# Key blocks 0 and 1 of the value matmuls behind the maxima's transpose, key blocks 2 and 3 with the sums at place 8 of 12

## The chip, the cores and the metric

The kernel runs on one core of one Trainium2 chip. The metric is the device time of one execution in microseconds (us), lower is better. Three runs of the kernel before gave 889.77, 891.34 and 891.32 us, with a median of 891.32 us.

## The reference, cut to what matters

One transformer layer on x of 4 x 512 x 1024 floats: layer norm, attention with 32 query heads of width 32 that share one key and one value head, a position bias and a causal mask, output projection, residual; then layer norm, a linear layer with unpacked integer weights, residual.

```python
q = (hidden_states @ Wq).reshape(b, s, NUM_HEADS, HEAD_DIM)
kv = hidden_states @ Wkv
k, v = (kv[..., :HEAD_DIM], kv[..., HEAD_DIM:])
scores = jnp.einsum('bqhd,bkd->bhqk', q, k) * scale
scores = jnp.where(causal[None, None], scores + bias[None], -jnp.inf)
attn = jax.nn.softmax(scores, axis=-1)
out = jnp.einsum('bhqk,bkd->bqhd', attn, v).reshape(b, s, h)
return out @ Wo
```

## The kernel before, in words

Three stages follow one another: projections of the four batches (to about 257 us of the profile), attention (about 257 to 570 us), and output projection with the linear layer, tile by tile. The change lies in attention.

Attention has 32 steps (`STEPS`), one for four heads of one batch. Each engine has its own program, written out by hand; a semaphore wait is the only thing that lets one engine wait for another, and each engine works through its list in order. In step s TensorE (PE) issues, in `attend(s)` (L644), twelve places (`RING`), 0 to 11:

- at every place but 2, one transposed score matmul (`score_t`, L609) into one of three PSUM banks of `p_st`, for step s. Places 0, 1, 3 and 4 are key block 0 of the four heads (512 columns), 5 to 8 key block 1 (384 columns), 9 and 10 key block 2 for two heads each, 11 key block 3 for all four (512 columns each). It waits until ScalarE has taken the exponential of the place three before it (`free_bank`, L585).
- at place 2, the transpose of the row maxima of step s+1 (`turn_max`, L599). It waits for the last maximum of that step and, as it uses the same three banks, for the exponential of place 11 of step s-1.
- after either, two, one or one plain score matmuls (`score`, L582) for the heads two steps ahead, of 128 and 256, then 384, then 512 columns. VectorE takes their row maxima (L948). Four scores make a head; a bank of `p_s` is written again once the maximum of the head before has been taken.
- at the places of two tables, the matmuls of step s-1 that multiply the exponentials by the values (`values`, L620, key block `kb`) and by the ones that sum them (`totals`, L633). These are plain fp32 matmuls with 32 columns of weights, in four column tiles at once (`128*32` in the profile, while all others show `128*128`). The profile shows eight records for four such instructions.

```python
VALUES_AT = {1: (0,), 4: (1,), 6: (2, 3)}
TOTALS_AT = {9: (0, 1)}
```

ScalarE (ACT) takes the exponentials of the eleven places in order (L789) into `pt`. Its program has three other operations in a step: the high part of the negated maxima (`max_high`, L781) between places 1 and 3, the copy of step s-1's output out of PSUM (`take_o`, L796) right behind the exponential of place 9, and in steps 2 to 17 one half-row cast of the output weights (`wo_high`, L805) right behind the exponential of place 10.

```python
if k == 8 and s > 0:
    take_o(s - 1)
if k == 9 and 0 <= s - 2 < HALVES:
    wo_high(s - 2)
```

VectorE (DVE) takes the sixteen maxima, then the low part of the transposed maxima (`max_low`, L955), the weights' low part (L965) in steps 3 to 18, and four reciprocals (L961), one behind each 256-column maximum, in steps 10 to 13, 18 to 21 and 26 to 29. GpSimd (POOL) cuts the exponentials at the diagonal (`cut`, L439) and adds key blocks before the sums (`add`, L446, L452). SyncE (SP) issues all DMAs in order: in each step the four loads of queries three steps ahead (`load_q`), the two stores of the maxima (`store_max`, L310, which the next step's first `score_t` waits for), the store of the output (`store_o`, L316, which waits for `take_o`), and one load of weights; in step 26 also five loads for the next stage.

Of the kernel before, what the change touches and what calls it, by code (L numbers as in the profile page):

```python
# [75 lines left out]
def layer(nc, x, wq, wkv, wo, qweight, w_scale, w_zero, bias, kpos, slopes, out, qh_d, ql_d, ext_d, wi_d, inv_d, o_d):  # L76

    ctx = ExitStack()
    with ctx:
# [433 lines left out]
        def _(pe):  # L513
# [98 lines left out]
            def values(s, kb):  # L612
                b = s // GROUPS
                if kb == 0:
                    at_least(pe, o_taken, s)
                    if s == 0:
                        pe.wait_ge(q_freed, CK * B + 2)
                pe.wait_ge(cut_done, 4 * s + kb + 1)
                for h in range(4):
                    last = pe.matmul(p_o[32 * h:32 * h + 32, kb * P:S], vst[:, TPB * b + kb, :],  # L620
                                     pt[s % 2][:, h, PT_AT[kb]:PT_AT[kb] + KB_LEN[kb]], start=(kb == 0), stop=(kb == 3),
                                     tile_position=(0, 32 * h), skip_group_check=True)
                if kb == 3:
                    last.then_inc(v_done, 1)

            def totals(s, part):
                b, g = s // GROUPS, s % GROUPS
                if part == 0:
                    at_least(pe, sums_taken, b if g == 0 else 0)
                    pe.wait_ge(add_done, 2 * s + 2)  # L630
                at, to = ((ADD_AT, slice(0, S)), (PT_AT[3], slice(2 * P, 3 * P)))[part]
                for h in range(4):
                    last = pe.matmul(p_sum[32 * h:32 * h + 32, to], pick[:, 7 - g:39 - g],  # L633
                                     pt[s % 2][:, h, at:at + to.stop - to.start], start=(g == 0 and part == 0),
                                     stop=(g == GROUPS - 1 and part == 1), tile_position=(0, 32 * h), skip_group_check=True)
                if part == 1:
                    last.then_inc(pv_done, 1)

            VALUES_AT = {1: (0,), 4: (1,), 6: (2, 3)}
            TOTALS_AT = {9: (0, 1)}  # L640

            FIRST_AT = {4: 0, 6: 1, 8: 2, 10: 3}

            def attend(s):  # L644
                n = 4 * (4 * s + AHEAD)
                for at in range(RING):
# [8 lines left out]
                    if s > 0:  # L655
                        for kb in VALUES_AT.get(at, ()):
                            values(s - 1, kb)
                        for part in TOTALS_AT.get(at, ()):
                            totals(s - 1, part)
# [468 lines left out]
```

## Time and profile before

| | us |
|---|---|
| median of three runs | 891.32 |
| lowest, highest run | 889.77, 891.34 |
| the profiled execution | 891.1 |
| its span, first to last instruction | 889.3 |
| TensorE busy | 850.5 (96%) |
| VectorE busy | 536.4 (60%) |
| ScalarE busy | 331.8 (37%) |
| GpSimd busy | 390.4 (44%) |
| mean granted TensorE clock | 0.991 |
| each step from 2 to 26, and 28 and 29 | 9.56 to 9.67 |
| steps 0, 1, 27, 30 | 10.80, 12.00, 10.90, 8.38 |
| step 18 (433.21 to 442.79): SP issues the maxima stores at | 436.82 and 437.37 |
| step 18: SP issues the output store at | 441.56 |

The span is that of the one profiled execution; 1.8 us of its time lie outside it. Busy shares are means over the three stages. The chain of waits is the work followed back from the last instruction. A step is read from the timeline: it begins where its first `score_t` starts. TensorE's records overlap, so the time that an instruction takes of the engine is the distance to the start of the next, not its own length.

### The profile page before, as it was taken

The numbers are of one execution on the slowest core, as the hardware profiler recorded it, in microseconds if no ns is written. First come the engines' busy times: TensorE is split into PE (matmuls) and PEld (weight loads), VectorE is DVE, ScalarE is ACT, GpSimd is POOL, SyncE is SP. The second block draws the span as 40 slices with busy tenths as digits, with TensorE's granted clock in tenths as the row PEclk, the third lists the DMA queues.
The fourth block names the chain that finished last, engine by engine and source line by source line (L and its number), as shares of the span: only waits on it lengthen the run. The fifth ranks groups of instructions, "written<-read, shape, count | busy, mean of one in ns | idle before, by whom it ended". The sixth has DMA issues, their size and how long they took to land.

```text
span 889.3 us, 13953 instructions
## 1 busy us (share of the span) xinstructions
PE 850.5 (96%) x4912; PEld 620.6 (70%) x4912; DVE 536.4 (60%) x1527; ACT 331.8 (37%) x647; POOL 390.4 (44%) x254
## 2 busy tenths in 40 slices
PE   2789999999989999999999999999999999999997
PEld 2578888888865555555555555578888888888885
DVE  6455253542575788888887777356655455555535
ACT  2323122222135767767766656422112112111211
POOL 1000000000016888888888888855443333444211
PEclk9989999999998999999999999999999999999999
DMA  5445554449443664666665572574344533334211
GB/s 160 145 157 154 166 160 145 138 133 219 137 119 89 154 150 124 153 145 142 147 150 154 157 182 76 156 187 119 96 117 130 127 100 107 95 95 117 73 48 48
DMA packets 90110, 117.19 MB, mean 132 GB/s; under 512 B 9060, under 2 KB 51044, under 8 KB 89960
## 3 DMA queue, kind: packets, MB, share of 16 engines
q1 hardware_dynamic: 90040, 116.30, 49.3%
q8 instruction: 39, 0.64, 0.3%
q14 instruction: 31, 0.25, 0.1%
HBM read 76.95 MB, written 38.93 MB: 130 GB/s over the span
## 4 chain that ended last, share of the span: by engine, by line
PE 89%; DVE 3%; DMA 3%; ACT 2%; SPq 1%; POOL 1%; issue 1%; DVEq 0%; ACTq 0%
PE p_o L529 19%; PE p_st L692 13%; PE p_s L677 10%; PE p_st L609 10%; PE p_o L677 9%; PE p_o L620 9%; PE p_s L582 9%; PE p_o L633 4%; PE p_st L529 2%; PE p_s L522 1%; DMA xt<-ml 1%; DMA raw<-in_wq_dram 1%; PE p_st L599 1%; PE p_s L706 1%; PE p_st L706 1%
## 5 line engine op out<-in xcount | busy, mean ns | idle before, releaser
L948 DVE CUSTOM_DVE_ANT_0 spill<-p_s,mask 128x128 bf16<-128x128 f32 (+3 forms) x512 | 224.2, 482 | 69.1 <-PE p_s L582 66.5
L439 POOL TENSOR_SCALAR_AFFINE_SELECT pt<-pt 128x512 f32<-128x512 f32 x128 | 83.1, 662 | 302.8 <-ACT pt L789 302.8
L789 ACT ACTIVATE pt<-p_st 128x512 f32<-128x512 f32 (+1 forms) x352 | 178.3, 560 | 90.5 <-PE p_st L609 90.2
L529 PE MATMUL p_o<-xt,wqh 128*128 128x512 f32 x512 | 170.1, 398 | 2.2 <-DVE wql L1058 2.2
L582 PE MATMUL p_s<-kst,xt 98*128 98x128 f32 (+3 forms) x512 | 149.7, 331 | 0.0
L609 PE MATMUL p_st<-xt,kst 100*128 100x512 f32 (+1 forms) x352 | 142.2, 408 | 6.1 <-DMA xt<-ml 4.6
L529 PEld LDWEIGHTS p_o<-xt,wqh 128*128 128x128 f32 x512 | 97.1, 190 | 22.8 <-DVE wql L1058 2.6
L446 POOL TENSOR_TENSOR pt<-pt 128x1536 f32<-128x1536 f32 x32 | 111.7, 3490 | 2.7
L582 PEld LDWEIGHTS p_s<-kst,xt 98*128 98x128 f32 x512 | 99.5, 195 | 11.9 <-DVE mx L948 0.9
L529 PE MATMUL p_o<-xt,wql 128*128 128x512 f32 x256 | 100.5, 392 | 0.0
L609 PEld LDWEIGHTS p_st<-xt,kst 100*128 100x128 f32 x352 | 66.9, 191 | 43.2 <-DVE ml L955 18.3
L462 POOL TENSOR_TENSOR osl<-ob,osh 128x1024 fp32r<-128x1024 f32 x14 | 33.6, 2403 | 134.2 <-ACT osh L825 134.1
L620 PE MATMUL p_o<-pt,vst 128*32 128x512 f32 (+3 forms) x1024 | 89.8, 445 | 0.0
L692 PE MATMUL p_st<-wi,yth 128*128 128x512 f32 x256 | 82.1, 397 | 2.2 <-DVE yo L1023 2.2
L692 PE MATMUL p_st<-wi,ytl 128*128 128x512 f32 x256 | 82.1, 397 | 0.0
L452 POOL TENSOR_TENSOR pt<-pt 128x1024 f32<-128x1024 f32 x32 | 76.4, 2387 | 0.0
L933 DVE TENSOR_TENSOR ql<-p_o,qh 128x512 fp32r<-128x512 f32 x32 | 22.1, 691 | 75.6 <-ACT qh L762 75.5
L762 ACT CAST qh<-p_o 128x512 fp32r<-128x512 f32 x32 | 18.8, 587 | 125.8 <-PE p_o L529 125.7
L469 POOL TENSOR_TENSOR xr<-xr,bias_b 128x1024 f32<-128x1024 f32 x16 | 50.6, 3161 | 30.8 <-ACT y L834 30.8
L692 PEld LDWEIGHTS p_st<-wi,yth 128*128 128x128 f32 x256 | 48.1, 188 | 14.1 <-issue 2.6
L842 ACT CAST yth<-p_s 128x512 fp32r<-128x512 f32 x16 | 9.4, 588 | 126.1 <-PE p_s L706 126.1
L692 PEld LDWEIGHTS p_st<-wi,ytl 128*128 128x128 f32 x256 | 48.2, 188 | 11.7
(104 smaller groups left out, 1205.1 us busy)
## 6 DMA issues: line engine op xcount, KB each, us to landing
xt<-qh_d SPq DMA_DIRECT2D x64, 256.0 KB
xin<-in_x_dram SPq DMA_DIRECT2D x16, 512.0 KB, 3.9
qh_d<-qh SPq DMA_DIRECT2D x32, 256.0 KB, 2.6
ql_d<-ql SPq DMA_DIRECT2D x32, 256.0 KB, 3.2
xt<-ql_d SPq DMA_DIRECT2D x32, 256.0 KB
o_d<-o_st SPq DMA_DIRECT2D x32, 256.0 KB, 2.8
ob<-o_d SPq DMA_DIRECT2D x64, 128.0 KB, 4.1
inv_b<-inv_d SPq DMA_DIRECT2D x64, 128.0 KB, 4.6
```

The source lines that it names most:

```text
L439: pool.affine_select(out=own, in_=own, compare_op=ALU.is_ge, fill=0.0, base=0, pattern=[[0, 4], [1, P]], channel_multiplier=-1).then_inc(c ...
L446: pool.tensor_tensor(p[:, :, ADD_AT:ADD_AT + 3 * P], p[:, :, PT_AT[0] + P:PT_AT[0] + S], p[:, :, PT_AT[1]:PT_AT[1] + 3 * P], ALU.add).then ...
L452: pool.tensor_tensor(to, to, p[:, :, PT_AT[2]:PT_AT[2] + 2 * P], ALU.add).then_inc(add_done, 1)
L469: pool.tensor_tensor(xr[:, t % 2, :], xr[:, t % 2, :], bias_b[:, :], ALU.add).then_inc(res_bias, 1)
L529: last = pe.matmul(dst, w[:, c, cols], xs[:, c, :], start=(c == 0 and k == 0), stop=(c == CK - 1 and k == 2))
L582: pe.matmul(scores_of(n), qst[s % 4][0:R_MAX, j, qb * P:(qb + 1) * P], kst[0:R_MAX, b * S:b * S + keys], start=True, stop=True).then_inc(s ...
L609: pe.matmul(p_st[:, place(k) % 3, 0:heads * KB_LEN[kb]], kst[0:R_END, b * S + kb * P:b * S + (kb + 1) * P], qst[s % 4][0:R_END, j:j + head ...
L620: last = pe.matmul(p_o[32 * h:32 * h + 32, kb * P:S], vst[:, TPB * b + kb, :], pt[s % 2][:, h, PT_AT[kb]:PT_AT[kb] + KB_LEN[kb]], start=(k ...
L677: last = pe.matmul(p_wo[t % 2][:, n, :], a[:, c, :], w[:, c, n * S:(n + 1) * S], start=(c == 0 and k == 0), stop=(c == CK - 1 and k == 2))
L692: last = pe.matmul(p_ff[:, n, :], a[:, c, :], wi[:, c, n * S:(n + 1) * S], start=(c == 0 and low == 0), stop=(c == CK - 1 and low == 1))
L789: act.activation(pt[s % 2][:, j:j + heads, PT_AT[kb]:PT_AT[kb] + KB_LEN[kb]], p_st[:, place(k) % 3, 0:heads * KB_LEN[kb]].rearrange("p (j ...
L948: dve.tensor_tensor_reduce(spill[:, SPILL_AT[qb]:SPILL_AT[qb] + keys], scores_of(n), mask[:, S - keys:S], 1.0, LOWEST, ALU.add, ALU.max, m ...
```

## The change

Two tables move the value matmuls and the sums to other places of the step. Nothing is added or removed.

```diff
-            VALUES_AT = {1: (0,), 4: (1,), 6: (2, 3)}
-            TOTALS_AT = {9: (0, 1)}
+            VALUES_AT = {2: (0, 1), 8: (2, 3)}
+            TOTALS_AT = {8: (0, 1)}
```

TensorE, places 0 to 4 of a step. L609 is `score_t`, L582 `score`, L620 `values`, L599 the transpose. Before:

```order
L609 MATMUL p_st<-xt,kst 128x512
L582 MATMUL p_s<-kst,xt 128x384
L620 MATMUL p_o<-pt,vst 32x512 x4
L599 MATMUL p_st<-ident,mx 128x128
L582 MATMUL p_s<-kst,xt 128x512
L609 MATMUL p_st<-xt,kst 128x512
L582 MATMUL p_s<-kst,xt 128x128
L582 MATMUL p_s<-kst,xt 128x256
L609 MATMUL p_st<-xt,kst 128x512
L582 MATMUL p_s<-kst,xt 128x384
L620 MATMUL p_o<-pt,vst 32x384 x4
```

The same places now:

```order
L609 MATMUL p_st<-xt,kst 128x512
L582 MATMUL p_s<-kst,xt 128x384
L599 MATMUL p_st<-ident,mx 128x128
L582 MATMUL p_s<-kst,xt 128x512
L620 MATMUL p_o<-pt,vst 32x512 x4
L620 MATMUL p_o<-pt,vst 32x384 x4
L609 MATMUL p_st<-xt,kst 128x512
```

The value matmuls of key block 0 stood ahead of the transpose and now stand behind it and the score that follows it; those of key block 1 come up from place 4.

TensorE, places 8 to 10, before (L633 is `totals`):

```order
L609 MATMUL p_st<-xt,kst 128x384
L582 MATMUL p_s<-kst,xt 128x512
L609 MATMUL p_st<-xt,kst 128x512
L582 MATMUL p_s<-kst,xt 128x128
L582 MATMUL p_s<-kst,xt 128x256
L633 MATMUL p_o<-pt,pick 32x512 x4
L633 MATMUL p_o<-pt,pick 32x128 x4
L609 MATMUL p_st<-xt,kst 128x512
```

Now:

```order
L609 MATMUL p_st<-xt,kst 128x384
L582 MATMUL p_s<-kst,xt 128x512
L620 MATMUL p_o<-pt,vst 32x256 x4
L620 MATMUL p_o<-pt,vst 32x128 x4
L633 MATMUL p_o<-pt,pick 32x512 x4
L633 MATMUL p_o<-pt,pick 32x128 x4
L609 MATMUL p_st<-xt,kst 128x512
L582 MATMUL p_s<-kst,xt 128x128
L582 MATMUL p_s<-kst,xt 128x256
```

Key blocks 2 and 3 leave place 6 and, with the sums, stand between the matmuls of place 8 and the `score_t` of place 9.

ScalarE's list is the same in both kernels. From the exponentials of places 5 to 8 on it reads, in steps 2 to 17:

```order
L789 ACTIVATE pt<-p_st 128x384 x4
L789 ACTIVATE pt<-p_st 128x2x256
L796 COPY o_st<-p_o 128x512
L789 ACTIVATE pt<-p_st 128x2x256
L805 CAST woh<-ob 128x512
```

The first `128x2x256` is place 9, whose `score_t` now comes behind the sums, and the copy of the output still follows it.

## Rows read from the trace of the kernel before

**Rows 1.** Window of step 18: length, busy PE, PEld, DVE, ACT, POOL; clock, DMA share, GB/s
```profile
433.20:442.78 9.58, 9.58 (x77) 5.67 (x76) 8.51 (x39) 6.74 (x15) 8.27 (x7) 1.00 0.61 143
```

**Rows 2.** Timeline of PE, step 18: start us, us, engine, line, operation, count
```profile
433.44 0.40 PE L582 MATMUL p_s<-kst,xt 98*128 98x128 f32 x2
433.68 0.41 PE L609 MATMUL p_st<-xt,kst 100*128 100x512 f32 x1
433.93 0.34 PE L582 MATMUL p_s<-kst,xt 98*128 98x384 f32 x1
434.19 1.06 PE L620 MATMUL p_o<-pt,vst 128*32 128x512 f32 x8
435.19 0.33 PE L599 MATMUL p_st<-ident,mx 128*128 128x128 f32 x1
435.27 0.48 PE L582 MATMUL p_s<-kst,xt 98*128 98x512 f32 x1
435.59 0.40 PE L609 MATMUL p_st<-xt,kst 100*128 100x512 f32 x1
...
438.36 0.86 PE L620 MATMUL p_o<-pt,vst 128*32 128x256 f32 x16
439.15 0.44 PE L609 MATMUL p_st<-xt,kst 100*128 100x384 f32 x1
...
440.59 1.28 PE L633 MATMUL p_o<-pt,pick 128*32 128x512 f32 x16
441.80 0.50 PE L609 MATMUL p_st<-xt,kst 100*128 100x512 f32 x1
442.13 0.34 PE L582 MATMUL p_s<-kst,xt 98*128 98x384 f32 x1
442.32 0.40 PE L609 MATMUL p_st<-xt,kst 100*128 100x512 f32 x1
442.55 0.40 PE L582 MATMUL p_s<-kst,xt 98*128 98x512 f32 x1
```

**Rows 3.** Timeline of DVE, around the start of step 18
```profile
433.05 0.56 DVE L948 CUSTOM_DVE_ANT_0 spill<-p_s,mask 128x384 bf16<-128x384 f32 x1 [0.95 <-PE p_s L582]
433.53 0.69 DVE L948 CUSTOM_DVE_ANT_0 spill<-p_s,mask 128x512 bf16<-128x512 f32 x1
434.14 0.29 DVE L948 CUSTOM_DVE_ANT_0 spill<-p_s,mask 128x128 bf16<-128x128 f32 x1
...
434.69 0.35 DVE L961 RECIPROCAL sums<-sums 128x32 f32<-128x32 f32 x1
434.96 0.50 DVE L948 CUSTOM_DVE_ANT_0 spill<-p_s,mask 128x384 bf16<-128x384 f32 x1
```

**Rows 4.** Timeline of all engines in step 0, a score that waits for a maximum
```profile
262.24 0.08 DVE L948 DVE_READ_ACCUMULATOR2_ANT mx<- 128x1 f32 x1
...
262.37 0.19 PEld L582 LDWEIGHTS p_s<-kst,xt 98*128 98x128 f32 x1 [0.31 <-DVE mx L948]
...
262.71 0.40 PE L609 MATMUL p_st<-xt,kst 100*128 100x512 f32 x1
```

**Rows 5.** Timeline of ACT, around the ends of steps 17 and 18
```profile
433.25 0.61 ACT L805 CAST woh<-ob 128x512 fp32r<-128x512 f32 x1
433.76 1.57 ACT L789 ACTIVATE pt<-p_st 128x512 f32<-128x512 f32 x3
...
440.95 0.58 ACT L796 COPY o_st<-p_o 128x512 f32<-128x512 f32 x1
442.33 1.09 ACT L789 ACTIVATE pt<-p_st 128x512 f32<-128x512 f32 x2 [0.80 <-PE p_st L609]
```

**Rows 6.** Chain of waits, 515 to 531 us (steps 26 and 27): start us, us, what
```profile
517.57 0.59 ACT o_st L796
...
524.30 6.05 DMA xt<-ml
```

**Rows 7.** Timeline of PE, the sums in step 30
```profile
556.20 1.28 PE L633 MATMUL p_o<-pt,pick 128*32 128x512 f32 x16 [1.13 <-POOL pt L452]
```

## The prediction

> **What bounds it now.** The page shows TensorE busy for 96% of the span. I read one step of attention next, by the sums over windows and the timeline. Step 18 takes 9.58 us, all of it busy on TensorE, with VectorE at 8.51, GpSimd at 8.27 and ScalarE at 6.74 [rows 1]. By the table above, the steps from 2 to 29 all take 9.56 to 9.67 us, except step 27 (10.90). So the step is TensorE's issue time, and what the others hold back is hidden, by 1.07 us in VectorE's case. Two questions decide: what the new order saves of the 9.58, and whether the two other engines, fed in larger lumps, still keep up.
>
> **What the order saves.** Durations are distances between starts [rows 2]. Plain matmuls cost 0.24 us for 512 columns (442.32 to 442.55), 0.18 for 384 (442.13 to 442.32), 0.24 for a 128 and a 256 together (433.44 to 433.68). A column-tiled group costs more than its columns: key blocks 2 and 3 (384 columns) take 0.79 (438.36 to 439.15), the sums (640 columns) 1.21 (440.59 to 441.80). The 256 columns between them cost 0.42, or 1.67 ns each, so each group has 0.15 fixed. The matmul ahead takes 0.08 more than its form (433.93 to 434.19, 0.26 for 0.18), the one behind 0.10 more (441.80 to 442.13, 0.33 for 0.24). That is 0.33 us for one group. Behind key block 0 stands the transpose, which with the slower start of its follower costs 0.17 (0.08 to 435.27, then 0.32 for 0.24). Now: four groups, 4 x 0.23 + 3 x 0.10 = 1.22, plus the transpose. After: two groups, 0.66. Both sides keep 0.17 for the transpose. **Saved: 0.56 us a step**, leaving 9.02 us of issue. Over 29 steps this is 16 us if nothing waits.
>
> The Trainium skill, TensorEngine Tiling (Array Packing), Key Properties, says that changing the tiling mode drains TensorE. That rule speaks for the change and its sign agrees with the fixed costs above.
>
> **What waits between places 3 and 8.** These six places now run without a pause: two heads of scores with six `score_t`. Count from the start of place 3. TensorE reaches the last score of place 8 after 0.33 (place 3, behind a group) + 0.24 + 0.24 + 0.18 + 0.18 + 0.24 + 0.18 + 0.24 + 0.18 + 0.18 + 0.18 = 2.37 us. It must wait for the 512-column maximum of the head before. VectorE starts on a score 0.31 us after it has streamed (the score at 442.13 has streamed at 442.32 [rows 2]; one step of 9.58 earlier that is 432.74, and VectorE starts at 433.05 [rows 3]) and its first pair here has streamed at 0.57. From 0.88 on it needs 0.55 for the pair (434.14 to 434.69), 0.48 for 384 and 0.61 for 512 columns (433.05, 433.53, 434.14) [rows 3], so the head is through at 2.52; reading the result takes 0.08, and TensorE goes on 0.05 later (262.24, 262.37) [rows 4], at 2.65. Wait 0.28. A waiting matmul also shows its weight load: from 262.37 to the next matmul at 262.71 are 0.34 for a form of 0.24 [rows 4], +0.10. **Cost: 0.4 us a step**, and 0.26 more where a reciprocal lies between (434.69 to 434.96 [rows 3]). In the old order two groups of 0.79 us stood here, and VectorE caught up in them.
>
> **What waits between place 9 and the next transpose.** Count from the start of place 9. Unhindered, TensorE reaches the transpose at 0.33 + 0.24 + 0.24 + 0.18 + 0.24 + 0.24 + 0.24 + 0.24 + 0.24 + 0.18 = 2.37 us. ScalarE used to take the exponential of place 9 and the output's copy (440.95) while TensorE did the sums, then sat idle for 0.80 us [rows 5]. Now place 9 comes behind the sums: ScalarE is idle during them, for 1.9 us of group, and starts at 0.53 (441.80 to 442.33). Then it has place 9, the copy, place 10, in steps 2 to 17 the cast, and place 11, at 0.49 us each (three take 1.57 and the last of them 0.60) and 0.51 for the cast (433.25 to 433.76) [rows 5]. Place 10 ends at 0.53 + 2 x 0.49 + 0.60 = 2.11, and place 1 of the next step needs its bank, where TensorE arrives at 1.95: with 0.05 to notice, 0.21 of wait and 0.10 of load, so the transpose would be reached at 2.68. Place 11 ends at 0.53 + 3 x 0.49 + 0.60 = 2.60, with the cast 3.11, and the transpose needs that: 2.65, or **3.16 with the cast**. VectorE allows it at 2.65, with a reciprocal 2.91. The old order hid this wait behind key block 0, which stood ahead of the transpose: VectorE was done at 434.14 + 0.08 [rows 3, 4], and the transpose came at 435.19 [rows 2]. So the loss is 0.31 us plain, 0.54 with a reciprocal, 0.79 with the cast.
>
> **By step** (a step pays for its own places 3 to 8, and at its transpose for the step before): plain, 9.02 + 0.38 + 0.31 = 9.71; with the cast 9.02 + 0.38 + 0.79 = 10.19; a reciprocal in places 3 to 8 adds 0.26, one ahead of the transpose 0.23 if there is no cast. Against 9.58:
> - cast alone, steps 3 to 9 and 14 to 17: 11 x 0.61 = 6.7
> - cast and reciprocals, 10 to 13 and 18: 5 x 0.87 = 4.4
> - reciprocals at both points, 19 to 21 and 27 to 29: 6 x 0.62 = 3.7
> - at one point, 22 and 26: 2 x 0.37 = 0.7
> - plain, 2 and 23 to 25: 4 x 0.13 = 0.5
> - step 1, whose transpose waits for nothing new: -0.2; step 0 has no groups and stays.
>
> Together +15.8 us.
>
> **Step 27 and the queues.** SP's list is unchanged, but its output store waits for the copy, which now ends about 1.6 us after place 9 starts, that is 0.15 us into the next step; before it ended at 440.95 + 0.58 [rows 5], 1.26 us ahead of it. The query loads behind it slip by about 1 us. Maxima stores are issued about 4 us into a step (the table), and the longest landing took 6.05 us [rows 6]; in steps of 10 us that is covered. It is not in step 27, where five more loads stand in SP's queue: from the copy's end at 518.16 to the landing at 530.35 are 12.2 us [rows 6], so the step lasts about 12.3 instead of 10.9. That is 0.8 beyond what it got above. GpSimd (8.27 of 9.58) gets the same spacing in longer steps, and its last sum for step s-1 is ready well ahead of place 8, so I cost it at nothing. Step 30 has no scores; its sums waited 1.13 us for GpSimd [rows 7], and now the copy and place 9 come behind them: +0.5 (bounds 0 and 1.5). In step 31 the projection pieces keep their places: 0 (bounds -1 and +1). Sum: **+17 us**, rounded. A larger load exposure is possible, since four matmuls in a step may pay it, some of them hidden in a later wait: I take +18.
>
> The profiled execution took 891.1 us (span 889.3), in line with the median of 891.32. Forecast: **909.0 us**, 2% slower. The skill's same page, under PSUM Bottleneck, warns that tiling speeds TensorE up but not the copies out of PSUM, which may become the bottleneck. No row can show that of tiling as such, yet it is the kind of limit that the sums find.
>
> **Rivals.** *All waits hidden.* If ScalarE and VectorE kept up as they do now, the 16 us of saved drains would be whole: 875 us. For it: TensorE is busy through all of step 18 [rows 1]. Against it: [rows 3, 5] put both engines' ends behind TensorE's arrival at three points. It decides the sign: below 0.56 us of waits a step the change is faster. 6%. By the skill's rule on drains alone the time would be about this one.
>
> *ScalarE has slack that I don't see*, and only VectorE's pace counts: 0.38 + 0.31 a step, 0.49 more in the twelve steps with reciprocals, gives 28 x 0.13 + 12 x 0.49 = +9.5 and the step 27 and 30 terms, about 902 us. For it: ScalarE is busy only 6.74 of 9.58. Against: the order of its list. 17%.
>
> *The maxima land late.* With the query loads next to the maxima stores, landing as late as 6.05 us after issue in every step, plain steps grow to 10.1 and others slightly, some 4 to 8 us more: 916 us. 12%.
>
> *My sum*, within 5 us: 62%. The last 3% are no change, where saving and waits balance.
>
> **Range and chances.** The terms' bounds (loads exposed or not, 0.1 us at two points of 29 steps, 6 us; step 30 and 31, 3 us) and the rivals on both sides give 900 to 918. Faster by over 0.2% (about what a measurement can tell from no change) 0.06, within 0.03, slower 0.91.
>
> **What would show it.** Right: steps near 10.2 us in 3 to 17 and 9.7 in 23 to 25; the transpose's weight load waiting for `pt` L789 in steps 3 to 18; scores of 512 columns at place 8 waiting for `mx` L948; ScalarE idle for 1.5 us or more ahead of place 9, not ahead of place 10; two groups a step with 0.15 fixed each. Wrong: steps of 9.1 to 9.3 us, or a transpose that waits for nothing.

## The result, and the profile after

The changed kernel takes 911.79 us (median of 4 runs, 908.19 to 912.85) where the kernel before takes 890.55 (4 runs, 889.52 to 891.34). The ratio is 1.0232, 95% interval 1.0201 to 1.0263: slower by 2.3%. The forecast was 909.0 us in a range of 900 to 918.

The profiled execution has a span of 906.4 us, 17.1 more than the one of before. The first lines of its page:

```profile
span 906.4 us, 13953 instructions
PE 860.4 (95%) x4912; PEld 620.6 (68%) x4912; DVE 528.7 (58%) x1527; ACT 320.2 (35%) x647; POOL 399.0 (44%) x254
```

The number of instructions is the same. The mean granted clock is 0.992, where it was 0.991, so the clock is no part of these 17.1 us. It is part of the distance between the medians, 21.2 us: the other three executions of the changed kernel have spans of 909.9 to 911.1 us at a mean granted clock of 0.987 to 0.989, and the span multiplied by the clock is 899.2 to 899.9 us in all four. The profiled execution is the fastest of them, and the remaining 4 us go with the clock.

The loss lies in attention, step by step. These are windows of four steps of the changed kernel: step 5 (with the weights' cast), 12 (cast and reciprocals), 21 (reciprocals) and 24 (neither). The columns are those of [rows 1].

```profile
309.86:320.19 10.33, 9.88 (x77) 5.71 (x77) 7.63 (x35) 6.32 (x15) 8.63 (x7) 1.00 0.56 132
382.60:393.15 10.55, 10.09 (x77) 5.61 (x77) 8.37 (x39) 6.38 (x15) 8.85 (x7) 1.00 0.52 128
475.97:486.15 10.18, 10.11 (x78) 5.69 (x77) 7.78 (x40) 5.86 (x14) 8.27 (x7) 1.00 0.54 134
505.95:515.78 9.83, 9.80 (x77) 5.49 (x77) 6.95 (x36) 5.80 (x14) 8.28 (x7) 1.00 0.60 152
```

All four were 9.58 us or within 0.02 of it. TensorE's busy column hides most of the loss: in the last of these steps it is 9.80 of 9.83 us, though the step is 0.25 us longer than before. A matmul that waits a little is drawn longer. The timeline of TensorE in step 5, which answers to [rows 2]:

```profile
309.86 0.40 PE L609 MATMUL p_st<-xt,kst 100*128 100x512 f32 x1
310.10 0.45 PE L582 MATMUL p_s<-kst,xt 98*128 98x128 f32 x2
310.58 0.50 PE L609 MATMUL p_st<-xt,kst 100*128 100x512 f32 x1
310.92 0.33 PE L582 MATMUL p_s<-kst,xt 98*128 98x384 f32 x1
311.67 0.30 PE L599 MATMUL p_st<-ident,mx 128*128 128x128 f32 x1 [0.42 <-DVE mx L948]
311.73 0.48 PE L582 MATMUL p_s<-kst,xt 98*128 98x512 f32 x1
312.14 1.71 PE L620 MATMUL p_o<-pt,vst 128*32 128x512 f32 x16
313.78 0.50 PE L609 MATMUL p_st<-xt,kst 100*128 100x512 f32 x1
...
316.12 0.34 PE L609 MATMUL p_st<-xt,kst 100*128 100x384 f32 x1
316.45 0.50 PE L582 MATMUL p_s<-kst,xt 98*128 98x512 f32 x1
316.88 0.86 PE L620 MATMUL p_o<-pt,vst 128*32 128x256 f32 x16
317.56 1.26 PE L633 MATMUL p_o<-pt,pick 128*32 128x512 f32 x16
318.75 0.50 PE L609 MATMUL p_st<-xt,kst 100*128 100x512 f32 x1
```

The two groups are there: 0.41 us from the score ahead to the first value matmul, then 1.64 (312.14 to 313.78) and 1.87 (316.88 to 318.75), with the fixed cost once each. Three waits are there too. At place 1 TensorE starts 0.48 us after the pair of scores (310.10 to 310.58) where the pair costs 0.24. The transpose comes 0.75 us after a score of 0.18 (310.92 to 311.67). The last score of place 8 comes 0.33 us after a `score_t` of 0.18 and costs 0.43 itself. What ends that last wait, in the timeline of all engines:

```profile
316.31 0.08 DVE L948 DVE_READ_ACCUMULATOR2_ANT mx<- 128x1 f32 x1
...
316.45 0.19 PEld L582 LDWEIGHTS p_s<-kst,xt 98*128 98x128 f32 x1 [0.31 <-DVE mx L948]
```

It is the maximum of the head before, read out at 316.39, 0.06 us ahead of the weight load: the same picture as in step 0 of before [rows 4], now in every step from 2 to 29. The scores of places 6 and 7 wait too, for 0.1 us or less (315.36 to 315.70 for a pair of 0.24), since VectorE is behind all along this stretch.

ScalarE's timeline around the end of step 4, against [rows 5]:

```profile
305.32 1.33 ACT L789 ACTIVATE pt<-p_st 128x384 f32<-128x384 f32 x3
308.95 0.60 ACT L789 ACTIVATE pt<-p_st 128x512 f32<-128x512 f32 x1 [2.29 <-PE p_st L609]
309.45 0.58 ACT L796 COPY o_st<-p_o 128x512 f32<-128x512 f32 x1
309.91 0.62 ACT L789 ACTIVATE pt<-p_st 128x512 f32<-128x512 f32 x1
310.40 0.63 ACT L805 CAST woh<-ob 128x512 fp32r<-128x512 f32 x1
310.90 1.60 ACT L789 ACTIVATE pt<-p_st 128x512 f32<-128x512 f32 x3
```

It sits idle for 2.29 us during the second group, then has place 9, the copy, place 10, the cast and place 11 in a row. In the kernel before it idled for 0.80 us behind the copy, with the copy done. The waits of steps 2 to 30 in sum (engine, line waited for: us, times, longest), and then the first two of the kernel before, steps 2 to 29:

```profile
ACT pt L789 <- PE p_st L609: 116.7, 60, 2.3
DVE spill L948 <- PE p_s L582: 72.2, 68, 1.6
POOL pt L439 <- ACT pt L789: 48.2, 58, 1.6
```

```profile
ACT pt L789 <- PE p_st L609: 74.0, 111, 1.1
DVE spill L948 <- PE p_s L582: 48.6, 84, 1.1
```

Two engines that wait 117 and 72 us for TensorE, more than before, still make TensorE wait: they idle while the groups run and are late when the scores come.

### The profile page after: what moved, and what is told of

Read it like the earlier page. It is cut to its first block, busy times and chain, and to the rows that moved or that the text cites. A ratio compares the mean times of both kernels' runs of the same rounds, so it can differ in the third digit from the quotient of the medians.

```text
span 906.4 us, 13953 instructions
## 1 busy us (share of the span) xinstructions
PE 860.4 (95%) x4912; PEld 620.6 (68%) x4912; DVE 528.7 (58%) x1527; ACT 320.2 (35%) x647; POOL 399.0 (44%) x254
## 4 chain that ended last, share of the span: by engine, by line
PE 84%; DVE 5%; DMA 4%; issue 3%; ACT 2%; SPq 1%; DVEq 0%; ACTq 0%
PE p_o L529 19%; PE p_st L692 13%; PE p_o L677 10%; PE p_s L677 10%; PE p_s L582 8%; PE p_o L620 8%; PE p_st L609 7%; PE p_o L633 3%; DMA xt<-ml 3%; PE p_st L529 2%; DVE spill L948 2%; PE p_s L522 1%; DMA raw<-in_wq_dram 1%; PE p_st L599 1%; PE p_s L706 1%
## 5 line engine op out<-in xcount | busy, mean ns | idle before, releaser
L948 DVE CUSTOM_DVE_ANT_0 spill<-p_s,mask 128x128 bf16<-128x128 f32 (+3 forms) x512 | 220.8, 482 | 90.9 <-PE p_s L582 90.1
L439 POOL TENSOR_SCALAR_AFFINE_SELECT pt<-pt 128x512 f32<-128x512 f32 x128 | 89.0, 707 | 313.5 <-ACT pt L789 313.5
L789 ACT ACTIVATE pt<-p_st 128x512 f32<-128x512 f32 (+1 forms) x352 | 175.7, 570 | 133.7 <-PE p_st L609 132.1
L582 PE MATMUL p_s<-kst,xt 98*128 98x128 f32 (+3 forms) x512 | 158.5, 349 | 0.1
L609 PE MATMUL p_st<-xt,kst 100*128 100x512 f32 (+1 forms) x352 | 141.5, 406 | 8.7 <-DMA xt<-ml 4.5
L582 PEld LDWEIGHTS p_s<-kst,xt 98*128 98x128 f32 x512 | 94.0, 192 | 29.4 <-DVE mx L948 19.2
L609 PEld LDWEIGHTS p_st<-xt,kst 100*128 100x128 f32 x352 | 66.5, 189 | 49.4 <-issue 25.7
L620 PE MATMUL p_o<-pt,vst 128*32 128x512 f32 (+3 forms) x1024 | 83.5, 443 | 0.0
L692 PEld LDWEIGHTS p_st<-wi,yth 128*128 128x128 f32 x256 | 48.2, 188 | 14.1 <-issue 2.6
L620 PEld LDWEIGHTS p_o<-pt,vst 128*32 128x32 f32 x1024 | 26.8, 110 | 41.0 <-issue 28.9
```

The costliest lines, as they stand in the source:

```text
L439: pool.affine_select(out=own, in_=own, compare_op=ALU.is_ge, fill=0.0, base=0, pattern=[[0, 4], [1, P]], channel_multiplier=-1).then_inc(c ...
L582: pe.matmul(scores_of(n), qst[s % 4][0:R_MAX, j, qb * P:(qb + 1) * P], kst[0:R_MAX, b * S:b * S + keys], start=True, stop=True).then_inc(s ...
L609: pe.matmul(p_st[:, place(k) % 3, 0:heads * KB_LEN[kb]], kst[0:R_END, b * S + kb * P:b * S + (kb + 1) * P], qst[s % 4][0:R_END, j:j + head ...
L692: last = pe.matmul(p_ff[:, n, :], a[:, c, :], wi[:, c, n * S:(n + 1) * S], start=(c == 0 and low == 0), stop=(c == CK - 1 and low == 1))
L789: act.activation(pt[s % 2][:, j:j + heads, PT_AT[kb]:PT_AT[kb] + KB_LEN[kb]], p_st[:, place(k) % 3, 0:heads * KB_LEN[kb]].rearrange("p (j ...
L948: dve.tensor_tensor_reduce(spill[:, SPILL_AT[qb]:SPILL_AT[qb] + keys], scores_of(n), mask[:, S - keys:S], 1.0, LOWEST, ALU.add, ALU.max, m ...
```

## Which engine holds the transpose

The profile puts the transpose's wait of 0.42 us down to a maximum of VectorE. My sum had put it down to ScalarE's exponential of place 11 in the steps with a cast. VectorE's timeline says when the last of the 16 maxima was ready:

```profile
310.33 0.69 DVE L948 CUSTOM_DVE_ANT_0 spill<-p_s,mask 128x512 bf16<-128x512 f32 x1
310.94 0.08 DVE L948 DVE_READ_ACCUMULATOR2_ANT mx<- 128x1 f32 x1
...
311.50 0.08 DVE L948 DVE_READ_ACCUMULATOR2_ANT mx<- 128x1 f32 x1
```

It was ready at 311.02, 0.65 us ahead of the transpose; place 11's exponential ended at about 310.90 + 0.62 = 311.52. Two semaphores, one label. VectorE had meanwhile gone on to the next head, and a maximum that the transpose does not need was read out at 311.58, just behind the exponential. That fits the label: it seems to name whichever semaphore went up last. In step 11, where a reciprocal delays that later maximum, the same wait carries ScalarE's name, as it does in steps 12 to 14:

```profile
373.88 0.30 PE L599 MATMUL p_st<-ident,mx 128*128 128x128 f32 x1 [0.41 <-ACT pt L789]
```

Theory S is my sum: ScalarE's list holds the transpose in steps 3 to 18, VectorE just behind it. Rival V believes the label. Rival L says that the late landings of the maxima make the loss. Three kernels tell them apart: the changed kernel with the copy moved, with the cast moved, and with both. Microseconds against the changed kernel are differences of medians from two sets of runs, in which the kernel before had 890.55 and 892.18 us (892.83 and 892.57 in the later sets), and the executions of one kernel differ by their clock. So they are good to 3 us at best; the step lengths, read from one trace each, are the sharper measure.

**The copy behind the exponential of place 8**

```diff
-                    if k == 8 and s > 0:
+                    if k == 7 and s > 0:
                         take_o(s - 1)
```

> The changed kernel with ScalarE's copy of the output moved from behind the exponential of place 9 to behind that of place 8, into its idle time during the value matmuls and sums. Theory S (the chain of ScalarE's list after place 9 holds the transpose in steps 3 to 18; without it VectorE's maxima hold it, 0.5 us earlier): steps 4 to 9 go from 10.33 to about 9.85 us, steps 11 to 13 from 10.54 to about 10.35, steps 23 and 24 stay at 9.8; the output store leaves earlier, so the late landings in steps 18, 25 and 27 go too. Time down by 8 to 11 us against the changed kernel. Rival V (VectorE's pace alone sets the transpose, as the profile's label on that wait says): steps 4 to 9 stay at 10.33. Rival L (late landings of the maxima make most of the loss): steps 4 to 9 stay, and only steps 18, 25 and 27 shrink, 3 us in all.

Measured: 900.89 us (4 runs, ratio to before 1.0090, 1.0069 to 1.0112), 10.9 us less than the changed kernel. Steps 4 to 9 take 9.84 or 9.85 us, steps 11 to 13 10.18 or 10.19, steps 23 and 24 9.77 or 9.78. Steps 18, 25 and 27 have lost their extra time (10.05, 9.77, 10.19). Its window of step 5, and then the timelines of TensorE, VectorE and ScalarE around the transpose:

```profile
309.24:319.08 9.84, 9.62 (x77) 5.61 (x76) 7.55 (x37) 6.44 (x15) 8.64 (x7) 1.00 0.58 136
```

```profile
310.56 0.30 PE L599 MATMUL p_st<-ident,mx 128*128 128x128 f32 x1 [0.22 <-ACT pt L789]
```

```profile
309.71 0.69 DVE L948 CUSTOM_DVE_ANT_0 spill<-p_s,mask 128x512 bf16<-128x512 f32 x1
310.32 0.08 DVE L948 DVE_READ_ACCUMULATOR2_ANT mx<- 128x1 f32 x1
```

```profile
309.81 1.58 ACT L789 ACTIVATE pt<-p_st 128x512 f32<-128x512 f32 x3
```

The two ends now lie within 0.02 us of each other: the maximum is read out at 310.32 + 0.08 = 310.40, place 11's exponential, the first of the three, ends at 309.81 + 0.60 to 0.62, about 310.42. Rival V is out: nothing on VectorE changed, and the step fell by 0.49 us, one copy. Rival L is out for these steps.

**The cast behind the exponential of place 8**

```diff
-                    if k == 9 and 0 <= s - 2 < HALVES:
+                    if k == 7 and 0 <= s - 2 < HALVES:
```

> The changed kernel with ScalarE's cast of the output weights moved from behind the exponential of place 10 to behind that of place 8. Theory S: steps 4 to 9 go from 10.33 to about 9.8, steps 11 to 13 to about 10.3, all steps from 19 on stay as they are, since they have no cast; time down by about 7 us. Rival V: steps 4 to 9 stay at 10.33, time unchanged. Rival L: nothing changes.

Measured: 905.14 us (ratio 1.0139, 1.0115 to 1.0163), 6.7 us less than the changed kernel. Most of steps 5 to 9 take 9.78 to 9.83 us, steps 11 to 13 10.10 to 10.19. Steps 20 and 21 are within 0.1 us of the changed kernel's. So far as expected; but steps 23, 26 and 28 took 10.33, 10.48 and 11.31 us in this execution (changed kernel 9.82, 9.90 and 9.67), where no change was expected. These are waits for the maxima's landing, and in step 28 also the clock, on which more below.

**Both**, that is, the two edits above together

> The changed kernel with both the copy and the cast behind the exponential of place 8. Theory S: no better than the copy alone (within 2 us of it), since VectorE then holds the transpose at 2.65 us after place 9 and either move takes ScalarE below that: steps 4 to 9 about 9.85. A rival in which ScalarE's list is the only limit: the two gains add, steps 4 to 9 go to about 9.4 us and the time by a further 7 us.

Measured: 898.69 us (ratio 1.0070, 1.0044 to 1.0097), 2.2 us less than with the copy alone; steps 4 to 9 take 9.77. The gains of 10.9 and 6.7 don't add: they end at the same wall, VectorE. In step 5 the maximum is read out at 310.09 + 0.08 = 310.17 and the transpose starts at 310.23, while place 11's exponential ended 0.5 us earlier; and steps with and without a cast are now equally long (9.77). A little over the 2 us that I had allowed is left; the steps account for 1.1 of them, 0.07 us in each step with a cast.

## VectorE's pace, and what the order really saves

**Reciprocals cut short**

```diff
-                of = slice(part * 32, part * 32 + 32)
+                of = slice(part * 32, part * 32 + (1 if b < B - 1 else 32))
```

> The changed kernel with the reciprocals of the first three batches cut from 32 columns to 1 (31 of 32 columns of the sums stay as they are, so the output differs). Theory S: VectorE's pace counts in places 3 to 8 and, without the cast, at the transpose: steps 11 to 13 go from 10.54 to about 10.4, steps 20 and 21 from 10.18 to about 9.9, steps 4 to 9 stay at 10.33. Time down 3 to 5 us. Rival (ScalarE alone): no step changes.

The kernel leaves out 31 of every 32 columns of these reciprocals. Measured: 908.50 us (ratio 1.0192, 1.0159 to 1.0224), 3.3 us less than the changed kernel. Steps 10 to 13 fall from 10.54 to 10.39 or 10.40, step 20 from 10.19 to 10.02, step 21 from 10.18 to 9.76; steps 4 to 9 stay at 10.33. VectorE does count, by these steps; the time alone would not show it, since the two ratios' intervals overlap, and the profiled span is 906.5 us, like the changed kernel's 906.4: steps 27 and 28 took 1.0 and 1.5 us longer here, by a later landing of the maxima and the clock behind it.

**Maxima over the last 128 keys only**, with copy and cast behind place 8. It leaves the other keys out of the row maxima.

```diff
-                keys = (qb + 1) * P
-                dve.tensor_tensor_reduce(..., scores_of(n),
+                keys = P
+                dve.tensor_tensor_reduce(..., scores_of(n)[:, qb * P:qb * P + P],
```

> The changed kernel with copy and cast behind place 8 and, besides, every row maximum taken over the last 128 keys only (the other keys are left out of the maxima, so the output differs). VectorE then needs about 0.2 us for each score in place of 0.2 to 0.6. Theory S (two groups in place of four save 0.56 us of issue a step, and waits for VectorE are all that is left in the way): steps of 9.0 us throughout, with at most 0.05 us between those with and without cast or reciprocals; time about 16 us below the kernel before (12 to 18). Rival (the drains that were counted as saved are paid elsewhere, or PE's own queue holds it): steps stay above 9.4 us.

Measured: 875.13 us (4 runs, 873.47 to 877.05; ratio 0.9799, 0.9776 to 0.9822), 17.4 us below the kernel before. Most steps take 8.93 to 8.96 us, with or without cast; the long ones are steps 2 and 26 (9.14 each), where the transpose waits for a maximum, steps 10 and 27 (9.36, 10.52), behind which TensorE idles for 0.27 and 1.42 us until the maxima land, and step 28 (10.68), of which more below. Against the kernel with both moves only the maxima differ, and step 5 falls from 9.77 to 8.95: those 0.82 us were VectorE's. The window of step 5, and TensorE around its transpose:

```profile
307.78:316.73 8.95, 8.95 (x77) 5.63 (x76) 4.81 (x35) 6.38 (x15) 8.24 (x7) 1.00 0.66 152
```

```profile
308.49 0.34 PE L582 MATMUL p_s<-kst,xt 98*128 98x384 f32 x1
308.66 0.27 PE L599 MATMUL p_st<-ident,mx 128*128 128x128 f32 x1
308.69 0.47 PE L582 MATMUL p_s<-kst,xt 98*128 98x512 f32 x1
309.09 1.71 PE L620 MATMUL p_o<-pt,vst 128*32 128x512 f32 x16
```

This is the saving with nothing in its way: 9.58 - 8.95 = 0.63 us a step, where I had worked out 0.56. The difference is the transpose. I had charged it 0.17 on both sides; between two plain matmuls it starts 0.17 after a score of 0.17 and its follower 0.03 later, and the next interval is 0.40, of which 0.24 are the score, 0.08 the lead into the group, 0.08 its own tail: 0.11 in all. The fixed cost belongs to the column-tiled groups, not to the transpose.

## Each half of the change alone

```diff
-            VALUES_AT = {2: (0, 1), 8: (2, 3)}
-            TOTALS_AT = {8: (0, 1)}
+            VALUES_AT = {2: (0, 1), 6: (2, 3)}
+            TOTALS_AT = {9: (0, 1)}
```

> The front half of the change alone: key blocks 0 and 1 at place 2, key blocks 2 and 3 at place 6 and the sums at place 9 as before. Theory S: one group less saves about 0.3 us a step, but the transpose now waits for VectorE and ScalarE (the copy is still done during the sums, so in steps with the cast for about 0.3 to 0.6 us, in others 0.2 to 0.4): steps 9.7 to 9.85 us, time 3 to 7 us above the kernel before. Rival (the back half alone makes the loss): steps of about 9.3 us, time 7 to 9 us below the kernel before.

Measured: 895.73 us (10 runs, ratio 1.0041, 1.0026 to 1.0056). Steps 4 to 9 take 9.82 to 9.84, steps 19 to 25 9.62 to 9.64.

```diff
-            VALUES_AT = {2: (0, 1), 8: (2, 3)}
+            VALUES_AT = {1: (0,), 4: (1,), 8: (2, 3)}
```

> The back half of the change alone: key block 0 at place 1 and 1 at place 4 as before, key blocks 2 and 3 with the sums at place 8. Theory S: one group less saves 0.33 us a step, but the copy now stands in ScalarE's list behind place 9 and after the sums; place 1 waits 0.2 to 0.3 us for the exponential of place 10, the transpose is hidden behind key block 0 as before except where the cast stands ahead of it, and places 5 to 8 run short of VectorE by 0.1 to 0.3 us: steps of about 9.6 to 9.8 us, time 3 to 8 us above the kernel before, with a late landing in step 27. Rival (the front half alone makes the loss): steps of about 9.25 us, time 9 us below the kernel before.

Measured: 901.04 us (4 runs, ratio 1.0105, 1.0072 to 1.0138), 8.2 above the kernel before in its own set of runs, just over the 3 to 8 that I had expected. Steps lie between 9.55 and 9.94 for the most part. Its weight loads name the landing of the maxima 13 times:

```profile
PEld p_st L609 <- DMA xt<-ml: 11.5, 13, 3.6
```

Late landings are not what this half loses by, though: steps without one (6 to 8, 18, 19) take 9.79 to 9.81 us, 0.22 more than before, which is 6 us over attention.

Each half loses, 0.4% and 1.1%, and the whole loses more than their sum (2.3%): with the front half alone the copy is still done during the sums, with the back half alone the transpose is still covered by key block 0. Together neither cover is left. This reading of the two halves is argued from the order of the lists; that each loses and that they more than add is measured.

**Key blocks 0 and 1 ahead of the transpose**

```diff
-            VALUES_AT = {2: (0, 1), 8: (2, 3)}
+            VALUES_AT = {1: (0, 1), 8: (2, 3)}
```

> As the changed kernel, but key blocks 0 and 1 stand at place 1, ahead of the transpose, and so hide its wait. Theory S: the transpose waits for nothing (its weight load is free 1.5 us before its turn), but place 3 onward still runs short of VectorE, now by a little more, since the group no longer lets VectorE finish the 512-column score of place 2, and ScalarE's copy still delays places 1 and 3: steps of 9.7 to 10.0 us without the step in time between steps with and without the cast being over 0.1 us, time 15 us above the kernel before (10 to 17). Rival (the transpose's wait is the whole loss): steps of about 9.1 us, faster than the kernel before by over 10 us.

Measured: 909.39 us (ratio 1.0191, 1.0155 to 1.0226), 16.6 above the kernel before; steps 6 to 9 take 10.01, like steps 22 to 24 without the cast (10.00 to 10.02). The transpose's wait is gone and so is the 0.5 us between steps with and without a cast. The loss is not: in step 22 TensorE's loads now wait at place 1 for ScalarE (0.22 us), at place 5 for the low part of the maxima, which comes behind the later transpose (0.59 us, with TensorE itself idle for 0.22), and at place 8 for a maximum (0.31 us). Steps 25, 27 and 28 took 11.37, 12.17 and 11.45 us, behind late landings of the maxima and, in step 28, at a lower clock.

## The maxima's landing

```diff
-                if s > 0:
-                    store_o(s - 1)
+                if s > 1:
+                    store_o(s - 2)
```

and `store_o(STEPS - 2)` behind the loop.

> The changed kernel with SP's output store of a step issued one step later, behind the stores of the maxima, so that neither the query loads nor the maxima wait for the copy. Theory S: the steps with waits for the maxima's landing (18, 25, 27 and 1.1 us in 27 as before) lose them: step 18 goes from 11.1 to about 10.5, step 25 from 10.7 to 9.8, step 27 from 11.3 to about 10.3; steps 4 to 9 stay at 10.33. Time down 2 to 3 us. Rival L (landing also holds the other steps): steps 4 to 9 fall below 10.2 and the time by over 5 us.

Measured: 908.76 us (ratio 1.0192, 1.0161 to 1.0222), 3.0 below the changed kernel, which is not clear of noise: the intervals overlap. Step 18 takes 10.52 where it took 11.11, step 25 9.81 for 10.73, step 27 10.19 for 11.34; steps 4 to 9 stay at 10.33. What stood in the changed kernel at the end of step 18, in the chain of waits and in TensorE's timeline, against [rows 6]:

```profile
448.99 7.10 DMA xt<-ml
```

```profile
456.13 0.50 PE L609 MATMUL p_st<-xt,kst 100*128 100x512 f32 x1 [0.40 <-DMA xt<-ml]
```

So rival L holds for three steps, not for the rest. What it is worth in sum is less than these steps show, 2.7 us: in the changed kernel the steps behind them, 19, 26 and 28, took only 9.66, 9.90 and 9.67, since ScalarE and VectorE caught up while TensorE stood; here they take 10.19, 10.17 and 10.18. That gives 1.3 us back, and 1.4 remain.

A long wait for the landing may cost a second time. In four of the kernels above (cast moved, reciprocals cut short, short maxima, key blocks ahead of the transpose) TensorE idled for 1.42 to 2.28 us ahead of step 28, and in the step that followed its granted clock fell. The window of the value matmuls of key blocks 0 and 1 in step 28, short maxima:

```profile
517.20:520.40 3.20, 3.20 (x18) 0.61 (x17) 0.92 (x8) 0.44 (x2) 2.04 (x1) 0.53 0.83 181
```

The clock is 0.53 there, nearly all of it at the lower of the two levels (1.2 GHz of 2.4); in the other three it is 0.50 for 3 us of step 28 or a little more. The group took 3.08 us (517.29 to 520.37) where it takes 1.64. Behind the 1.22 us of idle time ahead of step 28 in the changed kernel the clock stayed at 1.00. Step 1 of every kernel, the one before too, follows a wait of over 3 us and has a clock of 0.73 to 0.81. That the wait brings the clock down is read from this coincidence; no run tried it by itself.

## Is there an order that gains?

If VectorE needs its time between scores, groups should be spread, not gathered. Three groups save the fixed cost of one (these lines stand in place of the two tables):

```diff
+            VALUES_AT = {1: (0,), 4: (1, 2, 3)}
+            TOTALS_AT = {9: (0, 1)}
```

> Three groups: key block 0 at place 1, key blocks 1 to 3 at place 4, the sums at place 9; nothing else differs from the kernel before. Theory S: one group less saves 0.3 us of issue, VectorE falls short in the longer stretch of places 5 to 9 for part of it: steps of 9.4 to 9.55 us, time 1 to 4 us below the kernel before. Rival (any merging of groups costs more than it saves, as both halves of the change did): steps of 9.7 us or more.

Measured: 891.62 us (10 runs; before 892.57, 24 runs; ratio 0.9985, 0.9967 to 1.0004): no difference that the runs can tell. Steps from 2 to 26 take 9.52 to 9.60, within what I had expected.

```diff
+            VALUES_AT = {3: (0,), 7: (1, 2, 3)}
+            TOTALS_AT = {11: (0, 1)}
```

> Three groups spread evenly: key block 0 at place 3, key blocks 1 to 3 at place 7, the sums at place 11. Theory S: each stretch between groups holds about one head and a third of scores, which VectorE takes while the groups run; ScalarE's copy behind place 9 still has its time. Steps of 9.3 to 9.45 us, time 3 to 7 us below the kernel before. Rival (the transpose, with no group ahead of it, waits as in the changed kernel): steps of 9.7 us or more.

Measured: 891.24 us (10 runs, ratio 0.9981, 0.9970 to 0.9993), 1.3 below the kernel before where I had expected 3 to 7. Most steps take 9.50 or 9.51, above the 9.3 to 9.45 that I had expected; one step (15) took 10.79. Without waits a step should take about 9.26, an estimate from the 8.95 of the short maxima and 0.31 for one group more. The next run differs in the copy's place alone; what its step 5 has above that estimate stands at the scores.

> As the three even groups (places 3, 7 and 11), with ScalarE's copy of the output behind the exponential of place 8. Theory S: the copy is not on the path here, so steady steps stay within 0.03 us of those without it, and only the output store leaves SP earlier, which shortens step 27 by some 0.5 us. Rival (the copy still matters wherever the groups stand): over 0.1 us a step gained.

Measured: 888.56 us (9 runs, 886.55 to 891.75; ratio 0.9964, 0.9948 to 0.9981), 0.4% below the kernel before. The steady step stays at 9.50 to 9.51, as expected, and step 27 takes 10.43 for 11.02. The window of step 5 and two of its waits over attention:

```profile
308.27:317.78 9.51, 9.51 (x81) 5.77 (x77) 8.07 (x34) 6.53 (x15) 8.24 (x7) 1.00 0.58 141
```

```profile
PEld p_st L609 <- ACT pt L789: 28.5, 34, 1.4
...
PEld p_s L582 <- DVE mx L948: 11.2, 56, 0.2
```

The second line costs time: the pair of scores at place 3 waits for a maximum and takes 0.43 us up to the value matmuls, where 0.32 would do, and the `score_t` ahead of it and the last scores of places 7 and 11 take 0.04 or 0.05 more than their form. The first does not: the load's idle time falls within the group of key block 0, which takes its usual 1.00 us.

This order and the kernel with short maxima both beat the kernel before. The second gains 2.0% because it takes work from VectorE: with both moves and full maxima the same order loses 0.7%. The number subtracted in a softmax cancels in the quotient, so a maximum over part of a row changes only how large the exponentials may get; my expectation's remark that the output differs holds for the exponentials, not for the quotient. Whether it may be used depends on how far scores outside the last 128 keys can exceed those inside, which no run here bounds for other inputs.

## Why the prediction was right, point by point

| term | predicted | measured |
|---|---|---|
| order without waits, a step | 9.02 us | 8.95 (short maxima) |
| step with the cast (3 to 9) | 10.19 | 10.33 |
| cast and reciprocals (11 to 13) | 10.45 | 10.53 to 10.55 |
| reciprocals only (20, 21) | 10.20 | 10.19, 10.18 |
| neither (23, 24) | 9.71 | 9.82, 9.83 |
| step 27 | 12.3 | 11.34 |
| whole, against the profiled span of 889.3 | +18 | +17.1 (medians +21.2) |

- *What the order saves*: 0.56 predicted, 0.63 measured. Mis-sized by the transpose, as told above. (The sum's 0.42 us for 256 columns is 1.64 ns each, not 1.67; it changes no term by more than 0.01.)
- *Places 3 to 8*: from the start of place 3 to the value matmuls I had 2.37 + 0.28 + 0.10 + 0.24 + 0.08 = 3.07; the timeline has 3.10 (313.78 to 316.88).
- *Place 9 to the transpose*: 3.16 predicted with the cast, 3.25 measured (from 318.75 to the transpose of step 6 at 322.00). The 0.1 more lies, as in step 5, between place 11's end (311.52) and the transpose (311.67): 0.15 us, where I had taken the 0.05 of [rows 4]. With the copy moved it is 0.14. Where the maximum comes last, as in step 5 with both moves, the transpose follows it by 0.06, so two semaphores alone don't make the delay; its cause stays open. The copy moved ahead took 0.49 us off, its cost in the sum. The sign that I had named, the transpose's weight load waiting for `pt`, did not show: the load carries VectorE's name throughout, and only in steps 11 to 14 does the matmul carry ScalarE's.
- *The rival "all waits hidden"* would have been right without VectorE's and ScalarE's limits: 875 us was its price, and 875.13 is what the kernel with short maxima takes. That the two agree so closely is luck: 0.07 us more saved in a step is offset by longer steps at the end. The fixed costs that it counts are real: two groups less save 0.63 us. The Trainium skill says that changing the tiling mode drains TensorE (TensorEngine Tiling (Array Packing), Key Properties), and the trace agrees with that sign. It only doesn't decide.
- *The rival "ScalarE has slack"* fell with the copy moved: 0.49 us a step.
- *The rival "the maxima land late"* came true in part. I had put it in step 27 alone; in the profiled execution steps 18 and 25 were also longer by it, 0.6 and 0.9 us, while step 27 waited less than I thought. The landing behind step 18 took 7.10 us, above the 6.05 that I had as the longest.
- *Step 30*: +0.5 predicted, 8.91 for 8.38 measured.
- *The total* is in part luck. Steps 2 to 18 lost 14.1 us where the sum has 11.2, steps 19 to 29 lost 4.7 for 5.7, and the stretches outside steps 0 to 30 came out 1.8 us shorter, for which the sum has nothing. The 1 us added for exposed weight loads stood on no row, and the measured median has some 4 us that go with the clock and were not in the sum.

## What to carry to other kernels

The price of a group of matmuls is its fixed cost, but its use may be the time that it gives to the engines that drain PSUM. Before gathering groups, follow each consumer through the longest stretch without one: if three banks or one head of buffers fill before it is through, the stretch waits for it however low its busy share is. Look also at what stands in a consumer's list behind the instruction that now comes late: here one copy of 0.49 us, done for free before, went onto the path in every step with a cast. In steps without one, where VectorE holds the transpose, moving it saves only 0.05 us.

## What the runs showed that I had not expected

A wait on two semaphores was put down to the engine whose part had long been done: the transpose's 0.42 us carried VectorE's name while ScalarE held it, as the copy's move showed. A transpose of 128 columns between plain matmuls costs 0.11 us, while a column-tiled group costs about 0.33 us beyond its columns. And the same 8 KB store of the maxima, which lands 4.1 us after its issue in the median of the kernel before, took 7.10 us at step 18 of the changed kernel, whose SP queue had issued the output store and five loads in the 4 us before it. Its median in the changed kernel was 5.5 us; with the output store behind the maxima it was 3.6, and the long waits were gone. And such a landing may cost twice: in the four kernels in which TensorE idled for 1.42 to 2.28 us ahead of step 28, it ran at half its clock for some 3 us of that step.
